# Pairing narrow matmul passes in the second graph convolution, with the adjacency rows split into 1000-byte pieces

## What is computed

```
def gin_conv(x, src, dst, eps, W1, ln_g, ln_b, W2):
    n = x.shape[0]
    agg = jax.ops.segment_sum(x[src], dst, num_segments=n)
    h = (1.0 + eps) * x + agg
    h = jax.nn.relu(layer_norm(h @ W1, ln_g, ln_b))
    return h @ W2
src, dst = (edge_index[0], edge_index[1])
h = gin_conv(x, src, dst, eps_down, W1_down, lng_down, lnb_down, W2_down)
x = layer_norm(jax.nn.relu(h + x + dir_emb[0]), ln1_g, ln1_b)
h = gin_conv(x, dst, src, eps_up, W1_up, lng_up, lnb_up, W2_up)
```

## Time and profile before

| | |
|---|---|
| median of 3 runs | 2877.63 us |
| the profiled execution | 2889.01 us, span 2886.9 us |
| the stage's matmuls (L938) | 350 of them, first start 804.7, last ends 883.0 us |
| TensorE waiting for adjacency rows in the stage | 6.4 us in 16 waits |
| rate of the DMA engines within 820 to 870 us | 243 GB/s, share 1.02 |

### The profile page before, as it was taken

The page is one execution under the profiler, slowest core; times in us unless marked ns, Lnnn a source line. Parts: engine busy times, 40 slices in busy tenths (PEclk is TensorE's granted clock), DMA queues, the critical chain, the costliest instruction groups (busy, mean ns, idle before and its releaser), DMA issues. The chain is left out here.

```text
span 2886.9 us, 44422 instructions
## 1 busy us (share of the span) xinstructions
PE 2124.0 (74%) x12655; PEld 1717.0 (59%) x12655; DVE 1501.7 (52%) x4181; ACT 768.4 (27%) x1572; POOL 341.2 (12%) x383
## 2 busy tenths in 40 slices
PE   7678886553595235887659789954999975899893
PEld 4356664442443135777636567744888865899793
DVE  4499995776603975000166612246999845111113
ACT  4345553220100020222224100004666630111110
POOL 0000001001100100343200000000000000233231
PEclk9899998775586555999879899986999965999996
DMA  2023333000091011334330043203222011622835
GB/s 57 10 82 125 123 115 114 0 0 8 0 229 49 0 40 49 117 120 133 93 71 0 6 112 96 65 13 94 54 60 59 22 45 66 222 89 89 262 104 148
DMA packets 112421, 226.81 MB, mean 79 GB/s; under 512 B 15726, under 2 KB 69728, under 8 KB 112233
## 3 DMA queue, kind: packets, MB, share of 16 engines
q1 hardware_dynamic: 97376, 190.92, 22.8%
q0 software_dynamic: 11712, 32.00, 3.5%
q10 hardware_dynamic: 3270, 3.20, 0.3%
HBM read 161.40 MB, written 64.67 MB: 78 GB/s over the span
## 5 line engine op out<-in xcount | busy, mean ns | idle before, releaser
L1565 PE MATMUL experts_ps_h<-experts_xt,experts_w 128*128 128x128 f32 x1952 | 258.5, 289 | 60.0 <-DMA experts_b<-in_L_ffn_b 30.9
L1565 PEld LDWEIGHTS experts_ps_h<-experts_xt,experts_w 128*128 128x128 f32 x1952 | 249.8, 203 | 79.7 <-DMA experts_w<-in_L_ffn_w 34.4
L2161 PE MATMUL gat_ps_o<-Y,gat_prob_t 125*125 125x256 f32 x1250 | 274.2, 379 | 0.0
L2161 PEld LDWEIGHTS gat_ps_o<-Y,gat_prob_t 125*125 125x125 f32 x1250 | 233.0, 188 | 33.8
L827 PE MATMUL adj_ps_w<-adj_one_k,adj_one_s 128*125 128x500 bf16 x1000 | 178.1, 304 | 81.5 <-DVE adj_one_k L758 58.1
L1575 PE MATMUL experts_ps_o<-experts_w,experts_hid 128*128 128x256 f32 x976 | 231.8, 381 | 0.0
L1851 PE MATMUL gcn_ps_a<-Yp,gcn_adj 125*125 125x512 bf16 x625 | 205.9, 382 | 19.8 <-DVE gcn_acc L1867 9.9
L1638 DVE TENSOR_TENSOR experts_hid<-experts_gate,experts_ps_g 128x512 f32<-128x512 f32 x65 | 44.7, 688 | 328.0 <-ACT experts_gate L1615 328.0
L1602 ACT ACTIVATE experts_xt<-experts_ps_t 128x256 f32<-128x256 f32 x122 | 46.9, 384 | 625.2 <-PE experts_ps_t L1552 568.0
L1575 PEld LDWEIGHTS experts_ps_o<-experts_w,experts_hid 128*128 128x128 f32 x976 | 176.8, 191 | 19.2
L827 PEld LDWEIGHTS adj_ps_w<-adj_one_k,adj_one_s 128*125 128x125 bf16 x1000 | 98.2, 138 | 131.5 <-DVE adj_one_k L758 59.1
(11 more groups left out here) (356 smaller groups left out, 3828.5 us busy)
## 6 DMA issues: line engine op xcount, KB each, us to landing
experts_w<-in_L_ffn_w SPq DMA_DIRECT2D x84, 512.0 KB
adjacency<-adj_tile SPq DMA_DIRECT2D x25, 683.6 KB
adjacency_t<-adj_tile_t SPq DMA_DIRECT2D x25, 683.6 KB
up_adj_t<-adjacency_t SPq DMA_DIRECT2D x25, 683.6 KB
gcn_adj<-adjacency SPq DMA_DIRECT2D x25, 683.6 KB
gat_cnt<-adjacency_t SPq DMA_DIRECT2D x25, 683.6 KB
experts_w<-in_L_ffn_W SPq DMA_DIRECT2D x32, 512.0 KB
combine_got<-pair SPq DMA_DIRECT2D x20, 560.0 KB
```

The source lines that it names most:

```text
L1565: last = nc.tensor.matmul(ps[b][:, h * 128:(h + 1) * 128], w[b][:, k, h * 128:(h + 1) * 128], xt[b][:, k, :], start=(k == 0), stop=(k == K ...
L2161: last = nc.tensor.matmul(ps_o[b][0:ROWS, 0:C], prob_t[:, s * ROWS:(s + 1) * ROWS], K.Y[:, s, :], start=(s == 0), stop=(s == TILES - 1))
```

## The change

The rows of a tile land in SBUF as seven pieces with a pitch of 512 values: six of 500 values (1000 bytes) and one of 125 (250 bytes). A tile takes four transfers in place of two, and its semaphore counts to 64. The tiles are worked in pairs: the seven matmuls of parts 1 and 2 for each of the two tiles (128 columns, `wide`), and then for each bank two matmuls with 64 columns of part 3 (`narrow`), the first tile's into partitions 0 to 63 and the second's into partitions 64 to 127. The zero columns are no longer multiplied. Both buffers of a pair are released together. Tile 24 is worked alone. The loops of TensorE are written out in a straight line.

```
@@ -915,7 +915,8 @@
     cuts = [(a, min(a + 500, NODES)) for a in range(0, NODES, 500)]
     with ExitStack() as st:
         m = Memory(nc, st, "up")
-        adj_t = [m.sb(f"adj_t{i}", (ROWS, NODES), BF16) for i in range(4)]
+        adj_t = [m.sb(f"adj_t{i}", (ROWS, len(cuts), 512), BF16) for i in range(4)]
+        whole = NODES // 500
         agg_t = m.sb("agg_t", (128, NODES))
         ps = [m.ps(f"ps{i}") for i in range(7)]
         arrived = [m.sem(f"in{i}") for i in range(4)]
@@ -924,21 +925,51 @@
 
         @block.sync
         def _(sp):
-            load_tiles(sp, adj_t, K.adj_t, arrived, used)
+            def load(t, c):
+                tile = K.adj_t[bass.ds(t, 1)].rearrange("t p n -> (t p) n")
+                rows_dma(sp, adj_t[c][:, 0:whole, 0:500],
+                         tile[:, 0:whole * 500].rearrange("p (n w) -> p n w", w=500), arrived[c])
+                rows_dma(sp, adj_t[c][:, whole, 0:NODES - whole * 500], tile[:, whole * 500:NODES], arrived[c])
+
+            for t in range(4):
+                load(t, t)
+            with sp.Fori(1, TILES // 4) as j:
+                for c in range(4):
+                    sp.wait_ge(used, j * 4 + (c - 3) + START)
+                    load(j * 4 + c, c)
+            sp.wait_ge(used, TILES - 4 + START)
+            load(TILES - 1, (TILES - 1) % 4)
+            for c in range(4):
+                sp.wait_ge(arrived[c], (TILES + 3 - c) // 4 * 64 + START)
 
         @block.tensor
         def _(pe):
             for i, (a, z) in enumerate(cuts):
                 zero_bank(nc, K, ps[i], z - a, start=True)
 
-            def tile(t, b, i):
-                pe.wait_ge(arrived[b], (i + 1) * 32 + START)
-                for half in range(2):
-                    for n, (a, z) in enumerate(cuts):
-                        last = nc.tensor.matmul(ps[n][:, 0:z - a], K.Yp[:, t, half * 128:half * 128 + 128],
-                                                adj_t[b][:, a:z], start=False, stop=False)
-                last.then_inc(used, 1)
-            four_by_four(pe, tile)
+            def wide(t, b, i):
+                pe.wait_ge(arrived[b], (i + 1) * 64 + START)
+                for n, (a, z) in enumerate(cuts):
+                    nc.tensor.matmul(ps[n][:, 0:z - a], K.Yp[:, t, 0:128], adj_t[b][:, n, 0:z - a], start=False, stop=False)
+
+            def narrow(t, b, n, a, z, lo):
+                return nc.tensor.matmul(ps[n][lo:lo + 64, 0:z - a], K.Yp[:, t, 128:192], adj_t[b][:, n, 0:z - a],
+                                        start=False, stop=False)
+
+            def pair(t, b, i):
+                wide(t, b, i)
+                wide(t + 1, b + 1, i)
+                for n, (a, z) in enumerate(cuts):
+                    narrow(t, b, n, a, z, 0)
+                    last = narrow(t + 1, b + 1, n, a, z, 64)
+                last.then_inc(used, 2)
+
+            for t in range(0, TILES - 1, 2):
+                pair(t, t % 4, t // 4)
+            wide(TILES - 1, 0, TILES // 4)
+            for n, (a, z) in enumerate(cuts):
+                last = narrow(TILES - 1, 0, n, a, z, 0)
+            last.then_inc(used, 1)
             for i, (a, z) in enumerate(cuts):
                 last = zero_bank(nc, K, ps[i], z - a, start=False)
             last.then_inc(summed, 1)
```

## The result

The changed kernel takes 2895.82 us (median of 11 runs, 2884.81 to 2902.76), the kernel before 2877.25 us (11 runs, 2868.95 to 2883.92). The ratio is 1.0064, with a 95% interval of 1.0047 to 1.0081: slower by 18 us, between 13 and 23. The forecast was 2883 us, 5 us more; the time lies inside the stated range of 2868 to 2899 and beyond the 0.3% of no change, in the class that had 0.36. The way was forecast rightly, but the loss is over three times the forecast one: that it lies in the range is owed to the breadth of the range, not to the sum.

What follows compares the result with a forecast made beforehand. The prediction took the tile loads to bound the stage: +3.9 us for the pieces and +1.35 us for the later first release, +5.2 us in sum, on 2877.63 gave 2883 us, with a range of 2868 to 2899.

Steps and rivals of the forecast that it cites:

- the class that had 0.36: The outcome that the changed kernel is slower by over 0.3%, given a chance of 0.36.
- The loads bound the stage, so fewer matmuls save nothing.: Tiles 8 to 24: transfers at 3.215 us a tile set the pace over TensorE's 2.70; saved on the path: nothing.
- Narrow passes side by side at 4.05 us a pair.: TensorE's matmuls of a tile pair: 4.05 us in place of 5.4, hidden by the loads.
- Pieces: 3.40 us a tile, +3.9 us.: Tile loads in 1000-byte pieces: 3.40 us a tile against 3.215, 3.9 us more over 21 tiles.
- The first release, +1.35 us.: Stage front: seven pairs of narrow matmuls delay the first buffer release and the restart of loads by 1.35 us.
- It fits with 0.9 us to spare: nothing.: Steady part: new data flows 3.8 us after a pair's second arrival, within 4.7 us of queued loads; no cost.
- The 4.7 us of queued loads: Loads still queued when the second tile of a pair arrives, claimed as 4.7 us of work.
- rival A: Steady part: narrow matmuls one after the other, late release starves the queue; +11.3 us, 2889; chance 0.23.
- its second, the clock: Rival A's other way: at 1.2 GHz a pair holds its buffers 2.7 + 2.7 us; 5.4 us in all.
- Rival B: Tile loads: small pieces run nearer 300 GB/s, -11.6 us with the restart, 2866; chance 0.17.
- Rival D: Tile loads: pieces cost toward 3.89 us a tile, +14.2 + 1.35 us, 2893; chance 0.15.

Runs made afterwards that it cites:

- e9: Kernel before with rows at a 6400-byte pitch in DRAM, loaded as six 1024-byte pieces and one of 106, starting on 256-byte boundaries; ratio 1.0012.
- e15: As e9, with the rows in DRAM shifted by 20 bytes so that no piece starts on a 256-byte boundary; ratio 1.0027.
- e10: Kernel before with whole rows at a 6400-byte pitch in DRAM, so that they start on 256-byte boundaries; 2883.02 us, ratio 1.0015.
- e2: Changed kernel's paired matmuls and release per pair, with the whole rows and two transfers a tile of the kernel before; 2886.1 us, ratio 1.0028.
- e5: As e2, with eight buffers in place of four; 2879.04 us, ratio 1.0001.
- e3: As e2, with narrow passes widened to all 128 columns, so one after the other; 2887.49 us, ratio 1.0031.
- e1: Changed kernel's loads (four transfers, 1000-byte pieces), with the matmul order and release per tile of the kernel before; 2891.81 us, ratio 1.0045.
- e8: As e5, with a tile's rows cut at 120 and 5 partitions in place of 112 and 13; 2896.06 us, ratio 1.0045.

## Why the prediction came out as it did

- *The loads bound the stage, so fewer matmuls save nothing.* Right. TensorE's waits for rows went from 6.4 to 22.0 us (25 or more were forecast), and the stage grew.
- *Narrow passes side by side at 4.05 us a pair.* Right at the full clock: 1.49 for seven wide, 1.51 for 14 narrow. At the low clock, which the term left out, it is twice that.
- *Pieces: 3.40 us a tile, +3.9 us.* That they cost was right, and the term too small: 3.606, +8.2. The row that priced it, combine_got, has pieces that start on boundaries, and the prediction said so and let it stand. The Trainium skill, "DMA: Bandwidth & Descriptors", section "How a descriptor splits into AXI transactions", gave +7 us by my estimate, with the starts as the reason. The runs e9 and e15 bear it out in kind (0.14 us a tile for 20 bytes). That its number came near the measured one is in part luck: it has the odd starts as the only cost, and they are shown for 0.14 of the 0.39 us. Pieces that start on boundaries cost 0.27 against whole rows that do (e9, e10), and the parts don't add up to one account.
- *The first release, +1.35 us.* The issue of the fifth tile moved from 810.30 to 812.45; 0.6 of that is the stage's later start. That leaves 1.6 us, near the forecast.
- *"It fits with 0.9 us to spare: nothing."* This step failed, and it is the larger part of the miss. It took the full clock and evenly spaced pairs for granted, 2.7 us from the second arrival to the release. At the low clock it was 4.8 to 5.5, and the engines ran dry for 0.8 to 2.8 us, four times. With whole rows this and the later first release make 7.9 us (e2), and with eight buffers they are gone (e5). The 4.7 us of queued loads were reckoned nearly right: the engines ran dry 3.9 to 5.4 us after the second arrival. It was rival A without its first condition, since the narrow passes did not run one after the other, and with its second, the clock, which the prediction priced at 3 x 1.8 us and left out of the sum. Its signs, gaps in the steady part and a clock of 0.50, are in the trace. That the full clock would have closed the gaps is my estimate from the trace and was not run; e3 shows that a release 4.1 us after the arrival is late at the full clock too.
- *Rival B*, faster loads by smaller pieces: out, no piece was faster than whole rows. *Rival D*, pieces near 3.89 us: half way.

The sum by measured terms: 7.7 for the pieces (e1) and 7.9 for the release, the first one included (e2), make 15.6 against 16.0 in the trace, and the medians differ by 18.6 with an interval of 13 to 23. No single rival had this: it is half of D and the clock's branch of A together, and the prediction never added the two.

## What to carry to other kernels

Where transfers bound a stage, ask of a change to the matmuls only when it gives buffers back: with four buffers, a release of two at once turned a steady stream of loads into bunches of four with a gap behind each. When matmuls are taken away from a stage that waits for loads, the waits grow, and the clock may fall in them: reckon the release at 1.2 GHz too (here 5.5 us in place of 2.9) before the cover is called enough. Price pieces by rows that start where these will start, not only by rows of the same length, and compare like with like: aligned pieces with aligned rows. And a head start for the loads pays only as far as buffers come free again: with all eight full, the first release sets the pace.

## What the runs showed of the hardware

- Two 64-column bf16 matmuls in different column halves, with stationary and moving operands of their own, run side by side: 14 take 1.51 us at the full clock and 2.81 at the low one. Their weight loads take 110 ns in the median, those of 128 columns 98.
- In the changed kernel TensorE's clock fell five times from 820 us on, each time in a wait of 2.0 to 3.3 us or within 0.9 us behind it, and not in one of 2.15 us; it was back at 2.4 GHz about when the release came. In e2 it also fell in a wait of 1.75 us. In e5 TensorE waits 18 times, for 2.0 us at most, and its clock is 1.00 from 810 to 880 us.
- Cutting rows of 6250 bytes into 1000-byte pieces took the loads from 3.215 to 3.606 us a tile; aligned 1024-byte ones took 3.246, 3.386 when moved by 20 bytes. Aligned whole rows took 3.23 and then 2.80 or less (one trace, e10).
- Cutting a tile's 125 rows at 120 in place of 112 took the loads from 254 to 220 GB/s (e5, e8).
